# Scanning the last batch of a Mamba block as a front of 384 and a back of 128 tokens instead of in halves

## The reference

```
xz = einsum(hidden, in_proj_w); x, z = halves of xz        # 1024 channels each
x  = silu(causal 4-tap conv of x + conv_b)
dt, B, C = x_proj_w @ x                                    # 16 states
delta = softplus(dt_proj_w @ dt + dt_proj_b)
h  = exp(delta * A) * h + delta * B * x                    # token after token, per channel and state
y  = sum over states of h * C + x * D;  y = y * silu(z)
x  = layernorm(hidden + out_proj_w @ y)
two experts of eight per token: w = softmax of the two best of gate_w @ x
out = layernorm(x + sum of w * (expert_w @ x + expert_b))
```

## Time and profile before

| | us |
|---|---|
| median of 3 runs | 2265.98 (2260.73 to 2267.17) |
| the profiled execution, its own time | 2266.23 |
| its span, first to last instruction | 2264.4 |
| busy: TensorE, VectorE, GpSimd, ScalarE | 2034.1, 1982.4, 1854.7, 1658.7 |

### The profile page before, as it was taken

One profiled execution on the slowest core, in us unless ns is written; L12 is line 12 of the kernel. 1 busy time (PEld: TensorE's weight loads), 2 busy tenths in 40 slices (PEclk: granted clock), 3 DMA queues, 4 the chain that ended last, 5 costly groups with the idle time before them and its releaser, 6 DMA issues. The chain is left out here.

```text
span 2264.4 us, 30428 instructions
## 1 busy us (share of the span) xinstructions
PE 2034.1 (90%) x8624; PEld 1202.6 (53%) x8624; DVE 1982.4 (88%) x2191; ACT 1658.7 (73%) x3074; POOL 1854.7 (82%) x1505
## 2 busy tenths in 40 slices
PE   8897679898899989999899999999899998779998
PEld 3454445555555555545555555645555555545543
DVE  5899989989999999899999999999899988989911
ACT  5767858767598867979588876989588875666534
POOL 2978999788998889889898889999898987786503
PEclk9897879989899999999999999999999999769999
DMA  5432142267754786557764687557854675566875
GB/s 168 160 103 70 38 145 78 92 210 225 242 134 126 229 290 181 138 170 234 278 172 111 203 263 254 119 176 229 293 149 127 202 240 212 136 200 215 294 268 121
DMA packets 222085, 412.79 MB, mean 182 GB/s; under 512 B 29880, under 2 KB 36152, under 8 KB 221920
## 3 DMA queue, kind: packets, MB, share of 16 engines
q1 hardware_dynamic: 180448, 322.36, 42.4%
q0 software_dynamic: 20496, 57.16, 12.4%
q10 hardware_dynamic: 20976, 31.33, 4.2%
HBM read 299.37 MB, written 85.72 MB: 170 GB/s over the span
## 5 line engine op out<-in xcount | busy, mean ns | idle before, releaser
L1784 ACT ACTIVATE dA<-delta,negA 128x512 f32<-128x512 f32 (+1 forms) x1146 | 714.5, 637 | 318.0 <-DVE hst L1976 255.4
L1925 POOL TENSOR_TENSOR hst<-u,Bbc 128x512 f32<-128x512 f32 x666 | 880.9, 1427 | 55.3 <-PE hTp L1334 37.4
L1976 DVE TENSOR_TENSOR_SCAN hst<-dA,hst 128x512 f32<-128x512 f32 x672 | 790.6, 1208 | 41.7 <-ACT dA L1784 35.7
L1334 PEld LDWEIGHTS hTp<-ident,hst 128*128 128x128 f32 x4096 | 500.5, 149 | 320.2 <-issue 167.2
L1334 PE MATMUL hTp<-ident,hst 128*128 128x128 f32 x4096 | 562.4, 289 | 99.1 <-DVE hst L1976 24.0
L1965 DVE SCALAR_TENSOR_TENSOR y<-hTp,Ct,y 128x1024 f32<-128x1024 f32 x463 | 585.5, 1265 | 55.1 <-PE hTp L1334 51.8
L1925 POOL TENSOR_TENSOR first_dbu<-u,Bbc 128x512 f32<-128x512 f32 x222 | 294.8, 1408 | 18.7 <-DVE hits L2057 13.8
L1976 DVE TENSOR_TENSOR_SCAN hst<-dA,first_dbu 128x512 f32<-128x512 f32 x224 | 263.4, 1208 | 16.9 <-issue 9.2
L1318 PE MATMUL bank<-wslot,hidT 128*128 128x512 f32 x512 | 248.2, 616 | 5.7 <-ACT zs L1666 4.1
L1318 PE MATMUL bank<-wslot,tokT 128*128 128x512 f32 x480 | 225.9, 597 | 11.4 <-ACT tokT L1686 11.3
L1318 PE MATMUL bank<-delta,tokT 128*128 128x512 f32 x480 | 226.8, 606 | 0.3 <-issue 0.3
(11 more groups left out here) (187 smaller groups left out, 2878.4 us busy)
## 6 DMA issues: line engine op xcount, KB each, us to landing
wslot<-in_w_expT SPq DMA_DIRECT2D x90, 1024.0 KB
Bbc<-b_scratch SPq DMA_DIRECT2D x113, 256.0 KB
wslot<-in_w_inT SPq DMA_DIRECT2D x26, 1024.0 KB
y<-scaled POOLq DMA_DIRECT2D x49, 512.0 KB
zs<-sorted_tokens ACTq DMA_DIRECT2D x91, 256.0 KB
sorted_results<-ysb SPq DMA_DIRECT2D x90, 256.0 KB
res<-in_w_expT SPq DMA_DIRECT2D x18, 1024.0 KB
gate_scratch<-zs SPq DMA_DIRECT2D x64, 256.0 KB, 2.0
```

The source lines that it names most:

```text
L1334: mm = nc.tensor.transpose(hTp[q % 2][:, tok(j)], hst[n % 2][:, j, start:start + P], ident[:, :])
L1784: nc.scalar.activation(decay_of(step, halved), delta[w.odd][:, j, cols], ACT.Exp, scale=negA[:, j, n:n + 1]).then_inc(exp_done, 1)
L1925: nc.gpsimd.tensor_tensor(dbu_row(n, j), u[w.odd][:, j, :], Bbc[n % 2][:, :], ALU.mult).then_inc(dbu_done, 1)
L1976: nc.vector.tensor_tensor_scan(hst[n % 2][:, j, :], dA[j % 2][:, :], dbu_row(n, j), 0.0, ALU.mult, ALU.add).then_inc(scan_done, 1)
```

## The change

The last batch is cut at token 384 (`FRONT` = 3 tiles) instead of 256, and the back is one tile (`BACK` = 1).

- Steps 0 to 127 scan 384 columns, with one decay to a PSUM buffer and one product to an instruction. Steps 128 to 255 scan 128 columns, with four decays to a buffer and four products to an instruction. The B rows come in 15 front transfers and 4 back ones, each for four states.
- There are 3 front tiles with 3 state sums a state, and 1 with one. Three front tiles are normed, routed and scattered beside the scans: `HALF_TILES` becomes 13, of which 5 run beside the scans and 8 behind.
- Behind the scans one token tile is left: one pass of rows, 8 dense products. Each loaded expert serves one product instead of two. Three tiles of sorted results are gathered instead of two.
- The last rows of batch 6 go into `hst[1]`. They wait for the last state to be turned and for batch 6's own results, no longer for the last sorted results, and the plan starts them after the last tile's `x1T`.
- The gate values of batch 7 (`next_z`) are asked for at rows 40 + 8k instead of 60 + 12k. Priorities and pace of the last batch's plan have new numbers, so the order of its pieces changes throughout; the plan's costs for the scans follow the new sizes.

```diff
-HALF_TILES = (TOP * L // 2 + NE * (P - 1)) // P
+FRONT = NT - 1
+BACK = NT - FRONT
+EARLY_TILES = NT // 2
+HALF_TILES = (TOP * FRONT * P + NE * (P - 1)) // P
...
+GROUP = 4
+FRONT_SUMS = (130, 133, 136)
+BACK_LOADS = {121: 0, 132: 1, 164: 2, 196: 3}
...
-LAST_DEN = [(t, e) for t in range(PAIR, NT) for e in range(NE)]
+LAST_DEN = [(t, e) for t in range(FRONT, NT) for e in range(NE)]
...
-        "fin": [("sp", 0.5, [(("gate", 1), "dve", 8), (("moeL", ALL_TILES - 2), "sp", 4), (("moeL", ALL_TILES - 1), "sp", 4)] if alone else ...
+        "fin": [("sp", 0.5, [(("x1T", NT - 1), "act", 0)] if alone else ...
-        "next_z": [("sp", 0.5, [(("yT", HALF * NT - 1), "pe", 0.1), (("row", 60 + 12 * k), "dve", 0)])],
+        "next_z": [("sp", 0.5, [(("yT", HALF * NT - 1), "pe", 0.1), (("row", 40 + 8 * k), "dve", 0)])],
...
-    return [2 * r for r in range(NH + 1)] + list(range(3 * NH, 2 * STEPS, NH)) if halved else list(range(0, STEPS, 2))
+    if not halved:
+        return list(range(0, STEPS, 2))
+    front = [ND * (n + 1) + r for n in range(NS) for r in (0, 2, 5)]
+    return [2 * r for r in range(NH)] + front + [STEPS + ND * (n + 1) for n in range(NS - 1)]
...
-SEG_EPI = Segment(by_urgency({"lz": 66977, "L0": -107229, ...}), 0.15,
+SEG_EPI = Segment(by_urgency({"lz": 190, "L0": 893, ...}), 1.51,
...
-            return (ysb + spare)[t if w.tail else t % 2][:, :]
+            return hst[1][:, t, :] if w.tail else ysb[t % 2][:, :]
...
         def decay_of(step, halved):
 
+            if halved and step >= STEPS:
+                return dA[step // GROUP % 2][:, tok(step % GROUP)]
             if halved:
-                return dA[step // 2 % 2][:, step % 2 * HL:(step % 2 + 1) * HL]
+                return dA[step % 2][:, 0:FRONT * P]
...
                         for k in range(2):
-                            sync.wait_ge(ys_stored[k], all_results(w.d, k, w.tail))
+                            sync.wait_ge(ys_stored[k], all_results(w.d, k, False))
+                            sync.sem_inc(seen_sp, 1)
+                        if w.tail:
+                            sync.wait_ge(hT_done, NB * (NS * NH))
...
+            def load_back_B(w, g):
+
+                act.wait_ge(dbu_done, w.b * (NS * ND) + products(NS - 1 + g if g < 2 else NS + 4 * (g - 1)))
+                act.dma_start(Bbc[g % 2][:, :].rearrange("p (n t) -> p n t", n=4),
+                              b_dram[w.b:w.b + 1, 4 * g:4 * g + 4, FRONT * P:L].broadcast_to((P, 4, BACK * P))).then_inc(b_loaded[g % 2], 16)
...
-                scans = max(step - 2, -1) if halved else step - 1
+                scans = step - GROUP if halved and step > STEPS else step - 1
...
-                    elif w.seg.halved and j % 2 == 0:
-                        k, cols = step // 2, slice(n // NS * HL, (n // NS + 1) * HL)
+                    elif w.seg.halved and step < STEPS:
...
+                        nc.gpsimd.tensor_tensor(half_dbu[step % 4][:, 0:FRONT * P], u[w.odd][:, j, 0:FRONT * P], Bbc[n % 2][:, 0:FRONT * P], ALU.mult).then_inc(dbu_done, 1)
+                    elif w.seg.halved and j % GROUP == 0:
+                        m, k = n - NS, (step - STEPS) // GROUP
...
+                        nc.gpsimd.tensor_tensor(half_dbu[k % 4].rearrange("p (k t) -> p k t", k=GROUP), u[w.odd][:, j:j + GROUP, FRONT * P:L],
+                                                Bbc[m // 4 % 2][:, tok(m % 4)].unsqueeze(1).broadcast_to((P, GROUP, BACK * P)), ALU.mult).then_inc(dbu_done, 1)
...
-                        dve.wait_ge(exp_done, w.b * (NS * ND) + (step // 2 * 2 + 2))
-                        dve.wait_ge(dbu_done, w.b * (NS * ND) + (step // 2 + 1))
+                        back = step - STEPS
+                        dve.wait_ge(exp_done, w.b * (NS * ND) + (step + 1 if back < 0 else step // GROUP * GROUP + GROUP))
+                        dve.wait_ge(dbu_done, w.b * (NS * ND) + (step + 1 if back < 0 else STEPS + back // GROUP + 1))
```

More of the change, by code:

```diff
@@ L423, in start_main @@
         what, cost = {"act": (("exp", r), exp_cost), "pool": (("dbu", r), dbu_cost), "sp": (("B", r), 0.5), "pe": (("part", r), part_cost),
-                      "dve": (("scan", r), (0.6 if halved else scan_cost) + (add_cost if r in part_number and r not in scaled_at else 0))}[e]
+                      "dve": (("scan", r), ((0.86 if r < STEPS else 0.38) if halved else scan_cost) + (add_cost if r in part_number and r not in scaled_at else 0))}[e]
         if halved and e == "act":
-            cost = 0.45
+            cost = 0.55 if r < STEPS else 0.36
+        if halved and e == "pool" and r < STEPS:
+            cost = 1.0
         if e == "dve" and r in part_number and r not in scaled_at:
@@ L449, in may_start @@
             here = [y for r, y, _ in rows["pe"] if r == row and y[0] in TURNED]
-            return added.get(row, 1e9) + 0.1 <= now and (len(here) < 2 or fine and row == parts[-1] and ended(here[-2], "act", 0.1))
-        if x[0] in ("logits", "logF") and x[1] % PAIR:
+            return added.get(row, 1e9) + 0.1 <= now and (len(here) < 2 or (fine or halved) and row == parts[-1] and ended(here[-2], "act", 0.1))
+        if x[0] in ("logits", "logF") and x[1] % FRONT:
             return True
@@ L482, in plan @@
             for x, cost, after in first:
-                if fine and halved and e == "act" and x in turns and not all(ended(y, "act") for y in turns[:turns.index(x)]):
+                if halved and e == "act" and x in turns and not all(ended(y, "act") for y in turns[:turns.index(x)]):
                     continue
@@ L964, in build @@
         gathered = [sem(f"gathered{t}") for t in range(NT)]
-        half_gathered = [sem(f"half_gathered{t}") for t in range(PAIR)]
+        half_gathered = [sem(f"half_gathered{t}") for t in range(FRONT)]
         out_ready = sem("out_ready")
@@ L1321, in state_part @@
             def state_part(b, q, halved, first, turns):
-                n, _, start = part_of(q, halved)
-                per = PAIR if halved else NH
-                if q % per == 0:
-                    pe.wait_ge(scan_done, b * (NS * ND) + (q // per + 1) * ND)
+                n, t, start = part_of(q, halved)
+                if halved and t in (0, FRONT):
+                    pe.wait_ge(scan_done, b * (NS * ND) + (STEPS if t else 0) + (n + 1) * ND)
+                elif not halved and t == 0:
+                    pe.wait_ge(scan_done, b * (NS * ND) + (n + 1) * ND)
                 if not (first and q < 2):
@@ L1385, in piece @@
                     return
-                s, v = w.bank(x if name != "logits" else ("gate", x[1] // PAIR))
+                s, v = w.bank(x if name != "logits" else ("gate", x[1] // FRONT))
                 ps = bank[s]
-                if share == 0 and not (isinstance(v, int) and v == 1) and not (name == "logits" and x[1] % PAIR):
+                if share == 0 and not (isinstance(v, int) and v == 1) and not (name == "logits" and x[1] % FRONT):
                     pe.wait_ge(bank_taken[s], v - 1)
@@ L1490, in piece @@
                     mm = accumulate(ps[:, :], lambda i: side[k % 2][:, tok(i)], lambda i: W[:, i, :], KD, share)
-                if share == w.seg.shares.get(name, 1) - 1 and not (name == "logits" and x[1] % PAIR < PAIR - 1):
+                if share == w.seg.shares.get(name, 1) - 1 and not (name == "logits" and x[1] not in (FRONT - 1, NT - 1)):
                     mm.then_inc(bank_full[s], 1)
@@ L1506, in last @@
             def last(w):
-                for q in range(NS * NH - PAIR, NS * NH):
+                for q in range(NS * NH - BACK, NS * NH):
                     state_part(NB - 1, q, True, False, w.turned_base)
```

152 lines of the change are left out of this document (83 added, 69 removed).

## The result

The changed kernel takes 2292.78 us (median of 4 runs, 2288.28 to 2298.86) beside 2263.36 for the kernel before on the same chip (4 runs, 2255.18 to 2267.17): a ratio of 1.0123, 95% interval 1.0095 to 1.0150, some 28 us slower. The forecast of 2253 was wrong in sign, and the time lies outside its range. It is rival B, the front's rows too late, and 15 us beyond the price of B.

The account below looks back on a forecast made before the run. From 2014 on, one long TensorE queue with 9 us of holes was taken to bind. Last sorted tile 2224.8 - 7 + 3 = 2220.8, plus 31 is 2251.8 of span, so 2253 us; 8-in-10 range 2236 to 2272.

Parts of the forecast that it names:

- rival B: Front's rows come too late beside the scans; TensorE idles 25 us before the front's tokens: 2278 us; chance 0.14.
- Part 1: TensorE around the last sorted tile: eight dense products fewer remove 27.5 us behind it, two sorted tiles add 7.7 ahead.
- Part 2: One token row, 9.2 us plus 0.95 of state transposes, moves beside the scans; costs TensorE's queue nothing if fed.
- bare parts: Front's chain up to its scatters landing, summed from projections, products, norm, gating, counting, placing and scatters: 65 us.
- Parts 3 and 4: Last batch's scans, decays, products: VectorE needs 3 us more, decay waits 2 (0 to 7); VectorE has the slack.
- Part 5: Behind the last sorted tile: a chain of store, gathers, norm, store ends 31 us after it, against 48.2 now.
- Part 6: Transfers behind the scans: demand of 68 us in 61; 3 us charged, between 0 and 11.
- Part 7: TensorE's holes up to the last sorted tile: 7 us of 42 credited as filled, between 0 and 21.
- break-even at 69 us: Length of the front's chain, from front's end to tokens, from which the late-front rival decides: 2138 - 5 - 2064.
- A: TensorE's holes take the work in: half of the 42 us filled, 14 more than credited, 2239 us; chance 0.18.
- C: Transfers bind behind the scans: 11 instead of 3 us charged there, 2261 us, within 0.3%; chance 0.20.
- D: The change does nothing, since dense products were hidden; given no chance of its own.

Follow-up runs that it names:

- after_den5: Changed kernel with five dense products ahead of the last sorted tile instead of seven, the last three waiting for it: 2287.49 us, 1.0101 of the kernel before.
- tiles_free: Changed kernel whose thirteen front sorted tiles take the batch before's tokens and experts, so need not wait for the front: 2274.85 us, 1.0025 of the kernel before.
- before_6dense: Kernel before with six of the eight dense products of token tile 2 left out, nothing else: 2264.00 us, 0.9986 of the kernel before.

## Why the prediction was wrong, point by point

**Part 1, tiles and products: right in number, wrong in place.** The forecast kept 5 dense products ahead of the last sorted tile and 3 behind. There are 7 and 1. Behind the tile a product is free, ahead of it each costs 3.43 us: 2 x 3.43 = 6.9 us. after_den5 gave back 5 by time and 5.2 by trace from the tokens on, with the caution above. The gain of 27.5 us was charged to the stretch behind the tile, where the end chain caps it anyway.

**Part 2, the row beside the scans: its cover was gone.** The sum charged nothing for the row, on the condition that TensorE is fed until the front's sorted tiles, and nothing for the front's chain from its first product to its scatters. This is the step that failed. The front's first product comes 48 us later than before, and the chain with a third row takes 86.8 us and not the 65 of bare parts that rival B was weighed by. TensorE's other work ends at 2139.2, the tokens come at 2171.25, and TensorE idles 17.8 of the 34.3 us up to 2173.5. tiles_free takes this wait away and gets 22 us back. That the row's 10.1 us as work cost nothing was not tested by itself.

**Parts 3 and 4, scans, decays, products: right.** 0.94 and 0.46 us a scan, as interpolated. The front's last scan is over 199.9 us after the first (2072.2), against 199.3 forecast. VectorE waits 4.8 us for decays in the front's scans (2 charged, 0 to 7) and for GpSimd not at all. GpSimd's 384 columns take 1.09 us in the record; 128 of them are 132.6 us of busy time, 1.04 each, nearer the lower end as taken. The last scan ends 272 us after the first, 10 sooner than the 2147 of the forecast; nothing hung on it.

**Part 5, the end chain: right.** 31 us forecast, 31.0 measured, and 29.9 to 31.9 in the seven other kernels where the old rows are gone from it and few products follow.

**Part 6, transfers: 3 us charged, none found in the changed kernel.** What the sum missed is that the transfers would not have the 61 us: the share was 0.12 from 2110 to 2130 and then 1.0 from 2200 to 2260. Even so TensorE waits for no weight block there. It does, for 4.4 and 5.2 us, only with three dense products ahead. What the old rows in the state buffer cost is one dense product that the plan moves ahead of the tile, and in the kernel before 2 us of waits for ScalarE; neither is in the sum. The slices reach 396 GB/s (2206 to 2216); the Trainium skill, Perfetto Trace Analysis, section "Roofline", puts the bound of a core's sixteen DMA engines at about 435 GB/s, and no slice read here shows more than 413.

**Part 7, holes: wrong in sign.** It credited 7 of 42 us. In TensorE's 393.9 us up to the last sorted tile 331.4 are busy, 62.5 idle, where the kernel before has 309.3 and 42.2. The hole at 1960 to 1980 did shrink as hoped (15.9 of 20 busy against 12.4), and a larger one opened behind it. This makes up the whole miss: the tile is 37.8 us later than forecast, 24 of them idle time (62.5 against 42.2 less 7 plus 3) and 13.5 busy time (331.4 against 309.3 plus 8.6), of which the two dense products are 6.9. The other 6.6 fit the records at the lower clock in and behind the hole, but no run isolates them.

**Rival B** had the mechanism, the place and nearly the price, and 14% of the chance. It put the tokens on TensorE at 2162 and the end of TensorE's other work at 2138. Measured: 2171.25 and 2139.2, or 2163.7 and 2131.7 with the 7.5 us of late start taken off. From there it gave 114 us to the end (2278 less 1.8 less 2162), and it was 125.9: 6.9 by the two products, the rest by one tile at the lower clock (5.24 us for 3.60 at 2192) and waits between the front tiles, none of them for weights. Three faults kept its chance low:

- The break-even at 69 us was set against "bare parts" of 65, added from rows of engines that had nothing else to do. With three rows it was 84 to 90 us in six kernels whose front tiles wait for it, whatever the order; with two rows and nothing to spare it was 74. It could be read from the trace before: 81.6 us for two rows, of which the prediction believed a third to be slack.
- The earlier trace rows were read wrongly in one point. The sum at 2007.09 is not the last one of the front: the first gate product starts at 2019.72 and has waited for a VectorE sum (0.66 us). The two errors, start and length, cancelled, so that 2157 for the last scatter is within 3 us (2162.2, less the late start).
- A hole of TensorE was priced as idle time alone. It also halves the clock for what lies in and next to it: the bias products take 5.46 us for six records (0.91 each) where the earlier trace rows has 1.98 for four (0.50 each). The Trainium skill, TensorE: Matmul & The Clock Gate, section "What's actually happening", has an idle array at half clock until it has been busy again, and the trace agrees (0.52 in the hole, 1.00 from 2176 to 2186, then 0.83 in the 10 us with a wait of 2.6 us, and 1.00 again).

**The accounts.** 2278 by B, 6.9 for the two products, 5 for clock and waits behind the hole, 2 for tokens that come at 2163.7 and not 2162: 2292, against a profiled run of 2298.9 less its late start of 7.5, 2291.4, and a median of 2292.8. The 5 us are what is left of the 125.9 and were not priced by a run, so the agreement is in part made.

**Rivals A, C and D.** A fell: nothing absorbed the holes. C did not come in the changed kernel (Part 6). D, that the dense products alone do nothing, is true as long as the old rows stand in the end chain (before_6dense, 3 us); the two parts pay only together.

## What to carry to other kernels

When a change lengthens the first part of a two-part pipeline, compare the time at which its results are ready with the time at which the bound engine runs out of other work, and take the chain between from the trace as it is, not as the sum of its instructions. Delay that point in the kernel before, by two sizes: it prices a late front before the change is written (25 us here, where the change lost 28), though part of that price can come from the place that the delayed work leaves empty. Before a difference between two planned kernels is put down to a resource, count what the plan has laid ahead of the critical tile: one product more or less was 3.4 us here and looked like a cost of transfers. Work removed from behind the critical tile is worth only what the next chain leaves, and two covers that hide each other must go together.

## What the runs showed of the hardware

A scan is linear in its columns from 128 to 512: 459, 729, 940 and 1208 ns at 128, 256, 384 and 512 (the first two with a start value). GpSimd's product of 384 columns is 1.09 us against 1.28 for 512, so as an estimate the record has a fixed part of a third to half a microsecond, by a line through 1.28 and either 1.09 or the busy time of 1.04. A float32 product in eight records takes 3.60 us at full clock, and 5.24 to 6.17 next to a hole. Not expected: that kernels whose instructions are the same up to there reach the last batch up to 15 us apart in their profiles, and the front's tokens, with the same order on TensorE, another 6 us apart.
